# Layer-norm and 8-bit quantization of the activations: range and rounding read from x in float32 instead of from the normalized bfloat16 copy

## The reference

```python
def _layernorm(x, axis=-1, eps=1e-5):
    m = jnp.mean(x, axis=axis, keepdims=True)
    v = jnp.var(x, axis=axis, keepdims=True)
    return (x - m) / jnp.sqrt(v + eps)

def _act_quant(x):
    scale = 127.0 / jnp.clip(jnp.max(jnp.abs(x), axis=-1, keepdims=True), 1e-05)
    xq = jnp.clip(jnp.round(x * scale), -128.0, 127.0) / scale
    return x + jax.lax.stop_gradient(xq - x)

# attention part, on xn: three 1024x1024 projections and a scan over the tokens
g, v, d = xn @ Wg + bg, xn @ Wv + bv, xn @ Wd + bd
h[t] = (0.001 + 0.998 * sigmoid(d[t])) * h[t-1] + sigmoid(g[t]) * tanh(v[t])
# feed-forward part, on xn: weights ternary, inputs quantized to 8 bits by row
gate = silu(_bitlinear(x, w_gate)); up = _bitlinear(x, w_up)
return _bitlinear(gate * up, w_down)

xn = _layernorm(x)
x = x + attention(xn) + ffn(xn)
```

## Time and profile before

| what | us |
|---|---|
| time of the kernel, median of 2 runs | 6350.26 (6342.52 to 6358.0) |
| the profiled execution | 6357.58 |
| its span, first to last instruction of the slowest core | 6354.8 |
| spans of the eight cores | 6283.6 to 6354.8 |
| DVE busy in the span | 2910.8 |
| PE busy in the span | 2241.5 |

### The profile page before, as it was taken

The page is one execution under the profiler, slowest core; times in us unless marked ns, Lnnn a source line. Parts: engine busy times, 40 slices in busy tenths (PEclk is TensorE's granted clock), DMA queues, the critical chain, the costliest instruction groups (busy, mean ns, idle before and its releaser), DMA issues.

```text
span 6354.8 us, 44124 instructions; the slowest of 8 cores (6283.6 to 6354.8 us)
## 1 busy us (share of the span) xinstructions
PE 2241.5 (35%) x9367; PEld 1065.3 (17%) x9490; DVE 2910.8 (46%) x4898; ACT 395.7 (6%) x676; POOL 600.2 (9%) x769
## 2 busy tenths in 40 slices
PE   0022222112211222222055555565555555556543
PEld 0011111112100111111022122222222222122211
DVE  2344444444534544444355444454444545444551
ACT  1100000000000000000010000000000000000000
POOL 0000000000000000000011111111111111111110
PEclk9975555556555555555587777877777877778777
DMA  4132221223122232222323333333333333333324
GB/s 90 63 96 81 78 70 51 76 80 108 54 72 74 73 89 90 65 76 69 112 90 86 92 87 91 93 84 91 90 89 92 85 93 90 88 89 96 85 76 134
DMA packets 678949, 538.10 MB, mean 85 GB/s; under 512 B 532208, under 2 KB 532240, under 8 KB 676640
## 3 DMA queue, kind: packets, MB, share of 16 engines
q1 hardware_dynamic: 620288, 335.94, 20.0%
q0 software_dynamic: 58400, 199.35, 10.2%
HBM read 356.60 MB, written 109.05 MB: 73 GB/s over the span
## 4 chain that ended last, share of the span: by engine, by line
SPq 30%; DVE 27%; DMA 19%; PE 12%; issue 8%; ACT 2%; POOL 1%; DVEq 1%; ACTq 0%; POOLq 0%
SPq L292 14%; SPq L424 11%; DMA pqs<-scr_pqF 5%; PE pb L888 4%; PE pb L884 4%; PE pb L794 3%; SPq L580 2%; DMA qcm<-scr_acc 2%; DVE x_grp L260 2%; DMA pbuf<-x 2%; DVE dvecs L377 2%; DMA x_grp<-x 2%; DMA sg_slab<-scr_acc 2%; DVE pbuf L908 2%; DVE x_grp L262 2%
## 5 line engine op out<-in xcount | busy, mean ns | idle before, releaser
L794 PE MATMUL pb<-wdr,pqs 128*128 128x512 bf16 x2005 | 649.1, 456 | 1386.3 <-DMA pqs<-scr_pqF 1029.4
L628 PE MATMUL pb<-wqu,wqg 128*128 128x256 bf16 x3072 | 485.5, 333 | 1672.9 <-DMA wqu<-scr_xn 1672.9
L888 PE MATMUL pb<-wqu,xqF_t 128*128 128x512 bf16 x2048 | 886.0, 433 | 199.8 <-DMA xqF_t<-scr_xqT 192.9
L884 PE MATMUL pb<-wqg,xqF_t 128*128 128x512 bf16 x1968 | 870.9, 443 | 41.2 <-DVE pbuf L908 41.2
L628 PEld LDWEIGHTS pb<-wqu,wqg 128*128 128x128 bf16 x3072 | 363.3, 120 | 1775.3 <-issue 1676.9
L908 DVE SCALAR_TENSOR_TENSOR pbuf<-pb,dvecs,epi 128x512 f32<-128x512 f32 x256 | 192.1, 751 | 1012.5 <-ACT epi L898 1004.6
L794 PEld LDWEIGHTS pb<-wdr,pqs 128*128 128x128 bf16 x2048 | 201.4, 107 | 1742.6 <-issue 1607.4
L646 DVE TENSOR_TENSOR epi<-epi 128x256 f32<-128x256 f32 x128 | 54.4, 425 | 702.8 <-ACT epi L643 691.1
L898 ACT ACTIVATE epi<-pb,dvecs 128x512 f32<-128x512 f32 x256 | 175.9, 687 | 2768.5 <-PE pb L888 2098.3
L596 PE MATMUL pb<-idf_sb,epi 128*128 128x128 f32 x256 | 80.3, 385 | 757.6 <-DVE carry L653 757.5
L884 PEld LDWEIGHTS pb<-wqg,xqF_t 128*128 128x128 bf16 x2048 | 231.1, 113 | 584.1 <-issue 422.4
(11 more groups left out here) (108 smaller groups left out, 2559.1 us busy)
## 6 DMA issues: line engine op xcount, KB each, us to landing
wdr<-scr_wdT SPq DMA_DIRECT2D x512, 256.0 KB, 3.0
pbuf<-wdown POOLq DMA_DIRECT2D x64, 512.0 KB, 5.6
pbuf<-wgate POOLq DMA_DIRECT2D x64, 512.0 KB, 4.7
pbuf<-wup POOLq DMA_DIRECT2D x64, 512.0 KB, 4.6
scr_pqF<-pqstage POOLq DMA_DIRECT2D x64, 512.0 KB, 4.2
pqs<-scr_pqF SPq DMA_DIRECT2D x1024, 32.0 KB, 2.6
pbuf<-x SPq DMA_DIRECT2D x32, 512.0 KB, 3.5
x_grp<-x SPq DMA_DIRECT2D x32, 512.0 KB, 6.1
```

The source lines that it names most:

```text
L628: e.matmul(o, l, r, start=st, stop=sp),
L794: e.matmul(o, l, r, start=st, stop=sp),
L884: e.matmul(o, l, r, start=st, stop=sp),
L888: e.matmul(o, l, r, start=st, stop=sp),
```

## The change

In the loop over the tiles of a group the normalized bfloat16 tile is still written, but the range and the rounding no longer read it. The row maximum and the row minimum are taken from x in float32, the mean is subtracted from both, the larger of max-mean and mean-min is multiplied by `rstd`, and the factor and the step follow as before. The rounding starts from x in float32 as well: its first operation subtracts the mean and multiplies by `rs2`, the product of `rstd` and the factor. Two free columns of `consts_sb` hold values between. The queues of PE, ACT, POOL and SP have the same instructions in the same order as before.

```diff
-        def emit_round_neg(src_ap, s_vec_ap, dst_ap, clip1=False, pre_wait=()):
+        def emit_round_neg(src_ap, s_vec_ap, dst_ap, clip1=False, pre_wait=(),
+                           ln_pair=None):
...
-            if s_vec_ap is None:
+            if ln_pair is not None:
+                op("v", lambda e, a=src_ap, mm=ln_pair[0], rr=ln_pair[1], o=tq:
+                   e.tensor_scalar(o, a, mm, rr, OP.subtract, OP.mult),
+                   wait=pre_wait)
+            elif s_vec_ap is None:
...
-                mx, mc, rec, sv = scal[:, 0:1], scal[:, 1:2], scal[:, 2:3], scal[:, 3:4]
-                op("v", lambda e, i_=xnb, o=mx:
-                   e.tensor_reduce(o, i_, AX.X, OP.max, apply_absolute_value=True))
-                op("v", lambda e, i_=mx, o=mc: e.tensor_scalar(o, i_, 1e-5, None, OP.max))
+                r1, r2, a1, sv = scal[:, 0:1], scal[:, 1:2], scal[:, 2:3], scal[:, 3:4]
+                a2 = consts_sb[:, 9:10]
+                mvec = meanall[:, idx:idx + 1]
+                op("v", lambda e, i_=xtile, o=r1:
+                   e.tensor_reduce(o, i_, AX.X, OP.max))
+                op("v", lambda e, i_=xtile, o=r2:
+                   e.tensor_reduce(o, i_, AX.X, OP.min))
+                op("v", lambda e, i_=r1, m_=mvec, o=a1:
+                   e.tensor_scalar(o, i_, m_, None, OP.subtract))
+                op("v", lambda e, i_=r2, m_=mvec, o=a2:
+                   e.tensor_scalar(o, i_, m_, -1.0, OP.subtract, OP.mult))
+                op("v", lambda e, o=r1: e.tensor_tensor(o, a1, a2, OP.max))
+                op("v", lambda e, o=r2, r_=rstdall[:, idx:idx + 1]:
+                   e.tensor_tensor(o, r1, r_, OP.mult))
+                mc, rec = a1, a2
+                op("v", lambda e, i_=r2, o=mc: e.tensor_scalar(o, i_, 1e-5, None, OP.max))
...
+                rs2 = consts_sb[:, 8:9]
+                op("v", lambda e, a=rstdall[:, idx:idx + 1], b=sv, o=rs2:
+                   e.tensor_tensor(o, a, b, OP.mult))
                 for pc in range(2):
                     qw = tuple(xq_xp_marks[2 * (g - 1) + tt]) if (g > 0 and pc == 0) else ()
-                    emit_round_neg(xnb[:, pc * 512:(pc + 1) * 512], sv,
+                    emit_round_neg(xtile[:, pc * 512:(pc + 1) * 512], None,
                                    pqstage[:, tt * D + pc * 512:tt * D + (pc + 1) * 512],
-                                   pre_wait=qw)
+                                   pre_wait=qw,
+                                   ln_pair=(meanall[:, idx:idx + 1], rs2))
```

## The result

The changed kernel takes 6433.83 us (median of 7 runs, 6431.59 to 6460.6) against 6349.26 us (median of 6 runs) for the kernel before: a ratio of 1.0139, interval 1.0123 to 1.0155, which is 78 to 98 us more, 88 by the ratio and 84.6 by the two medians. The forecast was 91.5 us more, 6442 us. The profiled execution took 6434.74 us; its page is of core 4, which was the slowest this time.

The account below looks back on a forecast made before the run. The prediction took a relay of waiting legs, not DVE's total, as the bound. Reductions 1.323, small operations 1.416 and rounding 0.120 give 2.859 us per tile, 91.5 us over 32 tiles: 6442 us, range 6415 to 6470.

Parts of the forecast that it names:

- The bound: In the group loop, a relay of four legs: DVE's quantization leg is on the path at full length; 6442 us, chance 0.88.
- this leg: Per group, the 29.1 us from DVE's start on x to SP's first store of `xnb`; forecast to grow to 34.8 us.
- the empty window: From 1339 to 1369 us PE, ACT and POOL have no instruction and the DMA share is 0.00.
- SP's sixteen waits: SP's queue waited 16 times for the last rounding operation, 565.6 us in all; forecast to become 657 us.
- PE's sixteen waits: PE waited 16 times for the transposes after the leg; these waits should grow by 91.5 us.
- The reductions: In the leg, two float32 reductions of 1.220 us replace one; the second adds 1.323 us per tile, pause included.
- The operations on 128x1: In the leg, five more small DVE operations per tile, 0.159 or 0.212 us each plus pauses: 1.416 us per tile.
- the formula of the Trainium skill: 58 cycles plus the columns at 0.96 GHz per DVE operation; it would price the change at 46 us, about 6396 us.
- The first operation of the rounding: In the leg, a second per-row scalar makes it 546 ns, 60 ns more, twice per tile: 0.120 us.
- The slack: Rival: DVE's waits for transposed weights in the m loop absorb the extra time; no change, about 6350 us; chance 0.05.
- The clock: Rival: longer rest keeps PE at 1.2 GHz in the m loop; half exposed 107 us on top, 6549 us; chance 0.05.
- The size: Over 32 tiles of 2.859 us each, 91.5 us more in all, about 6442 us for the median.

Follow-up runs that it names:

- pair of kernels with the same work on either side of the mark: Kernel before plus six unread DVE operations per tile, ahead of or behind `vq_done`, which SP's stores wait for: 1.0147 ahead, 0.9997 behind.
- the run with the range alone: Against the kernel before: maximum and minimum from float32 x with their small operations, rounding still from the bfloat16 tile; 1.0119, 76 us more.
- rounding alone: Against the kernel before: rounding from float32 x with mean and `rs2`, range still from the bfloat16 tile; 1.0018, 11 us more.
- doubling the work: Kernel after plus six unread DVE operations per tile ahead of the mark `vq_done`; 1.0290 against the kernel before, 184 us more.

## Why the prediction was right

The forecast was 6442 us, 91.5 more; measured were 6434, and 78 to 98 more by the ratio. The steps, one by one:

*The bound.* "What the change adds to this leg adds to the span at its full length" rests on three readings, the empty window, SP's sixteen waits and PE's sixteen waits. The pair of kernels with the same work on either side of the mark shows it: 93 us ahead, none behind (at most 4). Before, DVE was busy 46% of the span, and after 46%. By that number nothing could have been said; by DVE's busy time alone both kernels of the pair would have been alike.

*The reductions.* Shown by the rows after (1220 ns twice) and by the run with the range alone, 76 us for the 79.4 of its terms.

*The operations on 128x1.* The ones with two tensors took 0.159 us as read; the two with a per-row scalar 214 ns where 212 had been estimated from the 59 ns that such a scalar costs on 512 columns. The estimate by the formula of the Trainium skill ("VectorE: DVE Perf Modes", the TRN2 errata), 46 us for the whole change, is outside the measured interval.

*The first operation of the rounding.* It took 546 ns as worked out; rounding alone cost 11 us for the 12.2 of its terms.

*The slack.* It is not there: DVE's waits for transposed weights and loads kept their size, and doubling the work doubled the cost.

*The clock.* It did not fall further: in group 6 the granted clock is 0.76 in the m loop before and after, and 0.50 in both rests ahead of it, and from 300 to 3200 us it is 0.60 in both kernels. The 3072 projection matmuls took 485.5 us before, 483.3 after and 488.5 with the doubled work, core 0; here is the row after, from 297 to 3270 us:

```profile
L649 PE MATMUL pb<-wqu,wqg 128*128 128x256 bf16 x3072 | 483.3, 332 | 1763.2 <-DMA wqu<-scr_xn 1763.2
```

That PE's clock was at its low level in the rest before the change too, so that a longer rest had nothing to take, fits this. The price of this rival was too high in any case: 8 x 1.67 us counts all eight bursts as fast, and in group 6 two of them took 3.91 and 4.45 us already before the change.

*The size.* The center of the measurement is 3 us below the sum by the ratio and 7 us by the medians. PE's wait for the transposes grew by 90.3 us on core 0, so the 91.5 is nearly all there in the attention stage. One core of one execution is no measure of the whole, though: the span of core 0 grew by only 58.1 us (6354.8 to 6412.9). Up to the first matmul of the feed-forward stage it had grown by 81.7 us (3205.0 to 3286.7), and the stage behind it, which the change does not touch, came out 23.6 us shorter. Over all eight cores the spans grew by 97.3 us on average. A difference of 3 to 7 us is less than what single executions of one kernel differ by, and is left open.

## What to carry to other kernels

Price an edit by the leg in which it stands: first find what the other engines do in that window, and if they all stand still and wait for this engine, every operation costs its duration and the pause behind it, whatever the engine's share of the span is. The same view shows the remedy: an operation that nobody waits for belongs behind the mark that releases the next leg, and a mark should be taken right behind the last operation that the next leg really needs. A statistic that needs a tile is cheaper at a place where the tile lies in SBUF and the engine waits anyway: here the two reductions cost 41 us in the statistics stage and 2 x 1.323 x 32 = 85 us in the leg.

## What the runs showed of the hardware

The price of a per-row scalar operand on DVE does not depend on the width: 59 to 60 ns on one column (214 against 154 ns), on 512 (486 against 427, and 546 with two of them), and on 1024 by the estimate in the prediction (812 ns measured with two, 693 estimated with none). The pause between two chained operations is 0.10 us behind a short one and behind a long one (3.3 us before 32 operations), with now and then one of 0.5 us; a program of many small operations pays it each time, 20 us of the 91.5 here.

Plain maximum and minimum over 1024 float32 columns take the 1220 ns of the sum and of the largest absolute value, and the largest absolute value takes the same from bfloat16.

Eight DMA transposes take 10.04 to 10.10 us on SP's queue (group 6 before, L292 from SBUF and L580 from DRAM); the 24 of a group are 30 of the 36 us between SP's first store and the first matmul.
